# Moving six of sixteen rescaling products from GpSimd to VectorE in a fused two-layer attention and FFN kernel

## The reference, cut to what matters

```python
scores = jnp.einsum('bqd,bkd->bqk', Q, K) / jnp.sqrt(jnp.asarray(hd, jnp.float32))
attn = jax.nn.softmax(scores, axis=0)
res = jnp.einsum('bqk,bkd->bqd', attn, V)
```

## Time and profile before

| | |
|---|---|
| median of 3 runs | 331.64 us (330.42 to 332.32) |
| time of the profiled execution | 329.17 us |
| its span | 327.0 us |
| PE busy | 311.4 us, 95% |
| DVE busy | 235.1 us, 72% |
| POOL busy | 159.8 us, 49% |
| ACT busy | 164.9 us, 50% |

### The profile page before, as it was taken

How to read it: one execution, slowest core, us unless ns; L and a number is a source line. 1 busy time by engine, 2 the same in 40 slices (tenths; PEclk the granted TensorE clock), 3 DMA queues, 4 the chain that set the end, 5 groups by cost and what they waited for, 6 DMA issues and landing times.

```text
span 327.0 us, 6054 instructions
## 1 busy us (share of the span) xinstructions
PE 311.4 (95%) x2060; PEld 240.2 (73%) x2060; DVE 235.1 (72%) x357; ACT 164.9 (50%) x279; POOL 159.8 (49%) x203
## 2 busy tenths in 40 slices
PE   4998999999999998999999999999999999599996
PEld 1896756767765565688988989897995577488884
DVE  3879787586577689655645646685599589999862
ACT  3854896556765567615326645265523444153330
POOL 5493640334032015101544161584988878769562
PEclk9599999999999999999999999999999999989999
DMA  7968987638911662021203333123451503000112
GB/s 213 352 194 146 183 173 158 107 124 138 152 34 43 106 96 70 11 88 34 58 24 93 106 77 106 37 63 100 145 154 43 181 21 111 2 2 30 62 71 96
DMA packets 32482, 32.71 MB, mean 100 GB/s; under 512 B 4252, under 2 KB 21660, under 8 KB 32454
## 3 DMA queue, kind: packets, MB, share of 16 engines
q1 hardware_dynamic: 32454, 32.34, 40.8%
HBM read 18.04 MB, written 2.10 MB: 62 GB/s over the span
## 4 chain that ended last, share of the span: by engine, by line
PE 72%; DVE 13%; DMA 6%; SPq 3%; ACT 3%; issue 2%; POOL 0%; ACTq 0%; DVEq 0%
PE ps L439 16%; PE ps L441 15%; PE ps L440 15%; PE ps L665 4%; PE ps L588 3%; DMA Q<-Q1d 3%; PE ps L654 3%; PE ps L633 3%; SPq L559 2%; PE ps L673 2%; PE ps L773 2%; PE ps L748 2%; DVE mx L1081 2%; DVE ps L1169 2%; DVE P L1179 2%
## 5 line engine op out<-in xcount | busy, mean ns | idle before, releaser
L1243 POOL TENSOR_TENSOR slot_l<-stg,slot_h 128x512 fp32r<-128x512 f32 x20 | 26.6, 1329 | 36.5 <-ACT slot_h L828 36.5
L1081 DVE TENSOR_REDUCE mx<-ps 128x8 f32<-128x1024 f32 x32 | 38.5, 1220 | 7.4 <-PE ps L633 7.4
L898 ACT ACTIVATE PT<-ps 128x1024 f32<-128x1024 f32 x32 | 32.2, 1027 | 16.0 <-PE ps L654 15.9
L1254 POOL TENSOR_SCALAR var_eps<-moments 128x1 f32<-128x1 f32 x32 | 8.5, 266 | 64.9 <-DVE moments L1044 64.0
L439 PE MATMUL ps<-xT_h,slot_h 128*128 128x256 f32 x128 | 36.8, 288 | 0.1
L441 PE MATMUL ps<-xT_h,slot_l 128*128 128x256 f32 x128 | 36.0, 281 | 0.0
L440 PE MATMUL ps<-xT_l,slot_h 128*128 128x256 f32 x128 | 35.9, 281 | 0.0
L1247 POOL TENSOR_TENSOR ctxT_l<-ctx_in,ctxT_h 128x512 fp32r<-128x512 f32 x14 | 18.1, 1295 | 19.4 <-ACT ctxT_h L835 19.3
L1098 DVE TENSOR_TENSOR X<-ps,X 128x512 f32<-128x512 f32 x24 | 16.4, 686 | 12.6 <-PE ps L441 7.4
L439 PEld LDWEIGHTS ps<-xT_h,slot_h 128*128 128x128 f32 x128 | 24.1, 189 | 1.7 <-issue 1.3
L851 ACT ACTIVATE xT_h<-ps 128x512 fp32r<-128x512 f32 x24 | 14.2, 597 | 21.8 <-PE ps L588 17.1
(11 more groups left out here) (159 smaller groups left out, 909.5 us busy)
## 6 DMA issues: line engine op xcount, KB each, us to landing
ctx_in<-in_ctx SPq DMA_DIRECT2D x22, 256.0 KB, 3.1
QS<-Q_h SPq DMA_DIRECT2D x32, 128.0 KB, 4.7
Q<-Q1d SPq DMA_DIRECT2D x64, 64.0 KB, 2.1
X<-in_x SPq DMA_DIRECT2D x8, 256.0 KB, 5.9
stg<-in_wq SPq DMA_DIRECT2D x8, 256.0 KB, 3.6
QS<-Q_l SPq DMA_DIRECT2D x16, 128.0 KB, 5.0
out<-XB SPq DMA_DIRECT2D x8, 256.0 KB, 2.0
stg<-in_wo SPq DMA_DIRECT2D x4, 256.0 KB, 3.3
```

The source lines that it names most:

```text
L898: act.activation(PT[:, g2, :], wide(step).rearrange("p k n -> p (k n)"), ACT.Exp, scale=SCALE0).then_inc(free(step), 1)
L1081: dve.tensor_reduce(mx[:, b % 2, :].rearrange("p (x r) -> p r x", r=REP)[:, r, :], wide(step).rearrange("p k (g t) -> p (k g) t", g=4), AX ...
L1243: pool.tensor_tensor(lo, src, hi.bitcast(F32), ALU.subtract).then_inc(w_lo_pool, 1)
```

## The change

The six products on GpSimd go to VectorE. They are put in VectorE's order at the place where the block that needs them has its other products. With no product left on GpSimd, the loop over `NMS_POOL` in FF emits nothing, so the six copies (L1174) are gone too. All other steps of all engines, and all sizes, are as before. Only two of the texts differ; of each a line is shown:

```diff
@@ DVE_TEXT
-S1.15 WE.0 FM.3 WE.1 WE.2 FZ.3 FF.3 CL.2.3 NM.14 WE.3 NM.13 FF.2 FF.1 NM.11 OX1.6 NM.8 NM.10 LNs.3.6 NM.5 OX1.7
+S1.15 WE.0 FM.3 WE.1 WE.2 FZ.3 FF.3 CL.2.3 NM.14 WE.3 NM.13 NM.12 NM.15 FF.2 FF.1 NM.11 NM.9 OX1.6 NM.8 NM.10
@@ POOL_TEXT
-CL.2.2 L.wbase.1 NM.12 NM.15 CL.2.0 NM.9 NM.6 CL.2.1 LNs.3.6 NM.4 LNs.3.7 L.wbase.2 XB.6 L.wbase.3 LNs.3.4 XB.7
+CL.2.2 L.wbase.1 CL.2.0 CL.2.1 LNs.3.6 LNs.3.7 L.wbase.2 XB.6 L.wbase.3 LNs.3.4 XB.7 LNs.3.5 XB.4 LNs.3.2
```

More of the change, by code:

```diff
@@ L107 @@
 Q1.12 S1.10 K1.12 Q1.13 K1.13 S1.11 FZ.1 Q1.14 FM.2 S1.12 WC K1.14 V1.6 S1.13 K1.15 Q1.15 FZ.2 CL.2.4 S1.14
-S1.15 WE.0 FM.3 WE.1 WE.2 FZ.3 FF.3 CL.2.3 NM.14 WE.3 NM.13 FF.2 FF.1 NM.11 OX1.6 NM.8 NM.10 LNs.3.6 NM.5 OX1.7
-FF.0 LNs.3.7 NM.7 XT.3.6 OX1.4 OX1.5 NM.0 LNs.3.4 XT.3.7 NM.3 OX1.3 NM.1 F1.6 LNs.3.5 F1.7 OX1.2 LNn.3.5 XT.3.4
-LNs.3.2 XT.3.5 OX1.0 LNs.3.3 F1.4 LNs.3.0 LNn.3.3 XT.3.2 OX1.1 LNs.3.1 XT.3.3 F1.5 LNn.3.1 F1.2 XT.3.0 F1.3
-XT.3.1 F1.0 F1.1
+S1.15 WE.0 FM.3 WE.1 WE.2 FZ.3 FF.3 CL.2.3 NM.14 WE.3 NM.13 NM.12 NM.15 FF.2 FF.1 NM.11 NM.9 OX1.6 NM.8 NM.10
+LNs.3.6 NM.5 NM.6 OX1.7 FF.0 NM.4 LNs.3.7 NM.7 XT.3.6 OX1.4 OX1.5 NM.0 NM.2 LNs.3.4 XT.3.7 NM.3 OX1.3 NM.1 F1.6
+LNs.3.5 F1.7 OX1.2 LNn.3.5 XT.3.4 LNs.3.2 XT.3.5 OX1.0 LNs.3.3 F1.4 LNs.3.0 LNn.3.3 XT.3.2 OX1.1 LNs.3.1 XT.3.3
+F1.5 LNn.3.1 F1.2 XT.3.0 F1.3 XT.3.1 F1.0 F1.1
 """
@@ L119 @@
 ZP.4 ZP.5 CL.1.7 CL.1.6 L.wv1.2 ZP.6 ZP.7 L.wv1.3 ZP.8 ZP.9 ZP.10 ZP.11 ZP.12 ZP.13 CL.2.5 ZP.14 ZP.15 L.wbase.0
-CL.2.2 L.wbase.1 NM.12 NM.15 CL.2.0 NM.9 NM.6 CL.2.1 LNs.3.6 NM.4 LNs.3.7 L.wbase.2 XB.6 L.wbase.3 LNs.3.4 XB.7
-NM.2 LNs.3.5 XB.4 LNs.3.2 LNs.3.3 LNs.3.0 XB.5 XB.2 LNs.3.1 XB.3 XB.0 XB.1
+CL.2.2 L.wbase.1 CL.2.0 CL.2.1 LNs.3.6 LNs.3.7 L.wbase.2 XB.6 L.wbase.3 LNs.3.4 XB.7 LNs.3.5 XB.4 LNs.3.2
+LNs.3.3 LNs.3.0 XB.5 XB.2 LNs.3.1 XB.3 XB.0 XB.1
 """
```

## The result

| | before | after |
|---|---|---|
| median, 22 runs each | 330.86 us | 329.48 us |
| profiled execution (span) | 329.17 us (327.0) | 327.67 us (325.5) |
| ratio after / before | | 0.9946, 95% interval 0.9922 to 0.9970 |

The ratio leaves out two of the changed kernel's 22 executions, which fell in a slower state of the chip; the medians don't. The ratio is 1.8 us (0.99 to 2.6) in favour of the changed kernel, against 1.9 us forecast; the medians lie 1.4 us apart. Two further measurements gave 0.9960 (0.9922 to 0.9997) and 0.9929 (0.9892 to 0.9966). The size is uncertain by about half.

A forecast was written before the change was run, and what follows sets the result against it. TensorE bounds the whole run, but VectorE's queue sets the pace in the rescaling stretch. VectorE's 1.33 us lead at F1.6 plus 0.54 slack gives about 1.9 us off 331.64: 329.7 us, range 327.9 to 332.0.

The forecast's parts named there:

- The long FF steps wait for GpSimd: FF.2, FF.1, FF.0 on VectorE: 10.71 us together, 1.05 each without a GpSimd product beside them; gives 7.56 us, copies included.
- Products and copies: VectorE's queue: six products of 1.13 us add 6.78 us; six copies removed save 1.24 us.
- The term of the copies: Six L1174 copies gone from VectorE, about 0.21 us each, two in FF.3 and FF.1, one in FF.2 and FF.0: 1.24 us.
- The handovers, walked through: VectorE's readouts: OX1.6 at 279.99, 2.43 us earlier; XT.3.6 at 290.66, 2.27 earlier; F1.6 at 298.98, 1.33 earlier.
- The last handover: OX1.2 on PE needs unit 2 from F1.6's readout: 1.33 us lead plus 0.54 slack, so PE keeps 1.87 us.
- The walk: VectorE's queue timed step by step from 269.90 us, 1.13 us per product and 0.60 per 128x512 instruction, to F1.6 at 298.98.
- lead of 2.25 us: PE from PV1.3 on, which waits for unit 0 from XT.3.6's readout: end 291.35 against 293.62, at either clock.
- The clock: 48 matmuls from PV1.4: 1.5 us instead of 2.8 if the clock stays up, but not kept, since PV1.2 and PV1.3 wait.
- The rival of a second fall behind 290 us: Second rival: granted clock falls to 0.50 in F1.6, PE loses 1.2 to 1.5 us; 0.7 to 1.0 arrive, 330.8 us; 18%.
- The sum: Whole run: 1.9 us saved off the median, 331.64 - 1.9 = 329.7 us, 0.57% faster.
- The other rivals: Third rival: CL.2.1 meets FF.1, or WE.3 its DMA, before OX1.6; 0.6 to 1.5 us arrive, 330.6 us; 12%.

The follow-up runs named there:

- the idle products: Changed kernel with five unread 128x1024 products, both inputs in SBUF, on GpSimd at the old places: 335.54 us, ratio 1.016 to the kernel before.
- The fills: Changed kernel with three zero fills of a dead tile on GpSimd at each place of the idle products: 330.15 us, ratio 0.9960 to the kernel before.
- the experiment: Changed kernel with the six copies of factors (L1174) left in, unread: 331.08 us, ratio 1.0004 to the kernel before.
- idle matmuls: Kernel before with ten idle 128x512 matmuls put before OX1.7 on PE, in its wait: 331.86 us, ratio 1.0031 to the kernel before.

## Why the prediction was right, point by point

- **The long FF steps wait for GpSimd.** Right. The steps shrank to 0.92 to 1.12 us where 1.05 was forecast, and the idle products brought the waits back with the same 0.15 and 0.55 us distances. The fills showed in addition that a busy GpSimd alone doesn't do it. The Trainium skill says as much ("SBUF — State Buffer", section "Who interferes with whom"): the VectorE instruction with two SBUF inputs contends with a GpSimd instruction that reads SBUF, not with one that only writes it. By that rule this case's traces agree, 0.28 and 0.70 us beside fills against up to 2.52 us beside a product.
- **Products and copies.** 1.13 us for a product was right: the three ahead of FF.2 take 272.58 to 275.97, 3.39 us. For four copies behind FF.2 the sum had 0.83 us, and the experiment gave 1.01. The sum took a copy's distance to the next instruction, 0.21 us, for its price. But a copy also needs the finished L1169: behind an L1169 of 0.70 us it begins 0.73 us after that one's start, where a product begins after 0.61. This 0.12 us was left out, once for each of FF.3, FF.1 and FF.0 (FF.2 is followed by the next L1167, and there the copy adds 0.15 in all). The term of the copies was too small by 0.3 us of 1.24.
- **The handovers, walked through.** The readouts of OX1.6, XT.3.6 and F1.6 came within 0.3 us of the times given, all slightly late, since the softmax's end lay 0.51 us later in this execution (L1159 at 268.55 against 268.04). Measured from there they were up to 0.4 us earlier than forecast.
- **The last handover was the wrong one.** This is the step that failed. The prediction had PE wait about 0.4 us before OX1.2 for the readout of F1.6. The trace shows 0.43 us before OX1.3, for the readout of XT.3.7, which holds unit 3, and none before OX1.2. The walk had XT.3.7 in its list but didn't ask which unit it frees. In the kernel before, that handover has these rows, of PE and of VectorE:

```profile
297.94 0.60 PE L784 MATMUL ps<-ident,O1T 128*128 128x128 f32 x4
296.68 0.66 DVE L1063 TENSOR_TENSOR xT_l<-ps,xT_h 128x512 fp32r<-128x512 f32 x1
```

By the walk's own numbers it bound harder. With OX1.3's readout at 297.25, behind NM.3 (1.13 us) and XT.3.7's own 0.60, XT.3.7's would begin at 295.52 and end at about 296.2, while PE with its lead of 2.25 us was ready for OX1.3 at about 295.7. The slack before was 297.94 - 297.34 - 0.06 = 0.54 us, and VectorE's lead 296.68 - 295.52 = 1.16, so PE would have kept 1.7 us and not 1.9.

- **So the 1.9 us were in part luck.** VectorE's lead was larger than the walk had it, by the copies that cost more: counted from L1159 it was 1.53 us at XT.3.7 (1.16 by the walk) and 1.73 at F1.6 (1.33). With the 0.54 us of slack that is 2.07 and 2.27 us, of which PE keeps the smaller. The two errors have opposite signs, 0.4 us too little lead and 0.2 us too much for the handover overlooked, and together they leave 0.1 to 0.2 us.
- **The clock.** Right that its recovery would not be kept. Before and after, with and without idle matmuls, PV1.3 begins when VectorE has read XT.3.6. The rival of a second fall behind 290 us didn't come about: the granted clock stayed at 1.00 through waits of 0.84, 0.17 and 0.43 us. In the trace with idle products PE waited 2.26 us before OX1.7, the clock was 0.50 to 0.54 from 289 to 292 us, and the stretch was still longer by VectorE's 3.04 us alone, so that fall was covered as well.
- **The sum.** 1.9 us forecast, 1.8 by the runs. By the traces it is 268.04 to 323.84 against 268.55 to 322.31, 2.04 us from L1159 to the last readout. It is made of 1.47 us behind CL.2.3's start, 0.41 for the two copies of FF.3, and 0.16 between the first L1169 and what follows it, 0.87 us before and 0.71 after. Of this 0.12 is the copy's wait again. The other 0.04 is chance: that L1169 took 0.84 us before and 0.80 after, both beside a GpSimd step, and 0.70 to 1.20 in other traces.
- **The other rivals.** CL.2.1 began on GpSimd at 278.77, 0.74 us after FF.1 was done, so they didn't meet. WE.3 met its DMA for 0.23 us in one trace of a variant, never in the three of the changed kernel.

## What to carry to other kernels

When an instruction of one form shows two durations in a trace, put the other engines' ends beside it: a fixed distance behind one engine's ends points at the cause, and idle work on that engine tests it. Work can be shared between VectorE and GpSimd if VectorE's part has one operand in PSUM; what must not lie beside GpSimd's reads are VectorE's instructions with two SBUF inputs. Moving all six products away was worth 0.5%. Leaving four of them on GpSimd, timed around the short steps, was worth 1.8% against the same kernel before, by six executions with an interval of 1.2 to 2.5%. And where buffers are handed over, walk through every one of them: what is kept is the smallest sum of lead and slack.

## What the runs showed of the hardware that was not expected

Whole runs of one kernel scatter by 1 to 2% although the stretch behind FF.2 repeats to 0.02 us. A part of that lies just ahead of it. In 8 of the 13 traces PE's granted clock falls to 0.50, 1.2 GHz, for 3.4 to 6.8 us somewhere between 261 and 272 us, during eight matmuls with 40 rows (the steps WE) or within 0.6 us of their end; in the other 5 it stays at 1.00 there. A window of the changed kernel's second trace, columns as in the earlier trace rows:

```profile
264.00:266.00 2.00, 2.00 (x5) 1.59 (x6) 0.63 (x2) 0.18 (x1) 1.84 (x4) 0.50 0.00 0
```

In that trace VectorE then waited for the context of V1.3:

```profile
272.38 0.69 DVE L1053 TENSOR_TENSOR ctxT_l<-ctx_in,ctxT_h 128x512 fp32r<-128x512 f32 x1 [1.08 <-ACT ctxT_h L835]
```

Where the clock fell, CL.2.3 waited for ACT like this in six of eight traces, by 1.07 to 3.21 us. From L1159 to CL.2.3 it takes 1.69 to 2.27 us in the five traces without the fall, 3.24 to 3.61 in the four with the shorter fall and 4.85 to 4.92 in the four with the longer one. This goes together with the fall; no run shows that the fall makes it. Another part lies further ahead: in the three traces of the changed kernel L1159 begins at 268.55, 269.12 and 270.92 us, the last of them without a fall anywhere before it.

The two sorts of traces don't divide by kernel: the changed kernel has one trace with the fall and two without. Nor do they divide by the wait of PE ahead of the steps WE, which was 0 to 1.52 us in traces with the fall and 0 to 1.65 us in those without. What decides it in an execution stays open; no run was made for it.
